# One-hot selection of the middle layers made by ScalarE in two steps, and the first block's factor held in PSUM, in a four-layer graph network

## The chip, the cores and the metric

The kernel runs on 1 core of one Trainium2 chip. The metric is the device time of one launch in microseconds (us). Engines are called by these names: PE (TensorE, matrix products), DVE (VectorE), ACT (ScalarE), POOL (GpSimd, which here issues the gathers of table rows) and SP (SyncE, plain DMAs).

## What is computed

A graph network of four layers over 3125 nodes (160 values each: 64 scalars and 32 vectors of 3) and 100000 edges, sorted by destination. Each layer normalises the nodes, looks up for each edge the row of a node, multiplies it by weights that a small network makes of the edge's attributes, and sums the messages over the edges that end at one node. The two middle layers are of one form; this is layer 2 (layer 1 has 8 attributes and no mean):

```
h = silu(edge_scalars @ (Wfc1 / sqrt(16)))
w = h @ (Wfc2 / sqrt(64));  w0, w1, w2, w3 = w[:, :64], w[:, 64:128], w[:, 128:160], w[:, 160:192]
e0, e1 = f0[edge_src], f1[edge_src]
sh0, sh1 = edge_attr_sh[:, :1], edge_attr_sh[:, 1:4]
mid0 = w0 * e0 * sh0
mid1 = w3 * einsum('eum,em->eu', e1, sh1) / sqrt(3)
mid2 = w1[:, :, None] * e0[:, :, None] * sh1[:, None, :]
mid3 = w2[:, :, None] * e1 * sh0[:, :, None]
n_k  = segment_sum(mid_k, edge_dst) / count
out  = sc + alpha * linear(n0..n3)
```

## The kernel before

Edges lie in tiles of 128 (one per partition); 4 tiles are a group, 2 tiles (half a group) are a unit whose destinations lie in one window of 128 nodes. Layer 0 runs 196 groups, then layers 1 and 2 run 208 groups each in a loop of their own (12 groups more than 196, for units that reach into a second window), then layer 3 has two passes. Between layers stand barriers of all engines. Everything is float32.

In the middle layers, for a group g:
- SP loads the edge attributes; POOL gathers 4 tiles of node rows from memory (`gathers_by_src`, line 567), up to 4 groups ahead (it waits until the messages of group g-4 are done).
- PE makes the hidden layer (`hidden_by_scalars`, line 1078, one product of 64x512) into bank 0; ACT takes it out with Silu (`hidden_out`, line 813); PE makes the weights w (`weights_by_hidden`, line 1092, four products of 192 columns) into PSUM, where each tile has 256 columns of which 192 are written.
- ACT multiplies the gathered rows by y0 (`rows_by_y0`, line 829, four instructions).
- DVE makes the one-hot selection (`select`: is the edge's place in its window equal to the column number, 128x512), the messages (`edges_by_window`, all recorded at line 1303), among them `t0` = w1 * e0 and the first block, `t0` times the three components of y (128x768), and adds the sums to the accumulator in SBUF (`add`).
- PE sums the messages over the window (`sums_by_window`, line 1111: per unit two products of selection and messages, 384 or 385 columns).

Each float32 product stands in the trace as two records, so 4 products of a group are x8.

The order of the work is written out by hand. `unrolled(count, [(lag, stage), ...])` runs, for each i, every stage on group i - lag, in the order of the list, and each engine executes its own list in order. The two lists that matter:

```
PE:  unrolled(ALL_GROUPS, [(0, sums_by_window(l)), (-2, weights_by_hidden(l)), (-3, hidden_by_scalars(l))])
ACT: unrolled(ALL_GROUPS, [(-1, rows_by_y0(l)), (-3, hidden_out(l))])
```

So in its turn i PE does the sums of group i, the weights of i+2 and the hidden layer of i+3; ACT does the rows of i+1 and takes out the hidden layer of i+3. Semaphores that the steps touch: `hidden_mm` (PE has made the hidden layer), `hidden_out` (ACT has taken it out), `weights_mm`, `rows_out`, `messages_done` (DVE), `sums_mm` (PE), `sums_added` (DVE), `got` (the gather has landed).

Of the kernel before, what the change touches and what calls it, by code (L numbers as in the profile page):

```python
# [87 lines left out]
def unrolled(count, stages):  # L88
    ahead, behind = min(lag for lag, _ in stages), max(lag for lag, _ in stages)
    for i in range(ahead, count + behind):  # L90
        for lag, stage in stages:
            if 0 <= i - lag < count:
                stage(i - lag)
# [7 lines left out]
def build(nc, a, out, layers=(0, 1, 2, 3)):  # L101
    with ExitStack() as ctx:
        def sb(name, shape, dt=F32):
            return ctx.enter_context(nc.sbuf_tensor(name, shape, dt))
# [27 lines left out]
        window_i = sb("window_i", [P, UNITS], I32)  # L132
        unit_i = sb("unit_i", [P, MORE], I32)
        column = sb("column", [P, P])
        put_i = sb("put_i", [P, TILES], I32)
        ident = sb("ident", [P, P])
        lower = sb("lower", [P, P])
# [45 lines left out]
        for l in (1, 2):  # L183
# [37 lines left out]
            "hid_free", "w_ready", "w_free", "weights_scaled", "msg_ready", "msg_free", "run_mm", "run_free",  # L221
            "run_ready",

            "scalars_in0", "scalars_in1", "hidden_mm", "hidden_out", "weights_mm", "rows_out", "messages_done",
            "sums_mm", "sums_added", "acc_zeroed", "acc_whole", "acc_turned", "acc_in_sbuf", "acc_mm", "acc_out",
            "p2_in0", "p2_in1", "p2_messages", "p2_mm", "p2_added",

# [45 lines left out]
        def window_views():  # L273
            g = carve()
            v = type("Windows", (), {})
            v.attr = g(2, 512)
            v.hid = g(2, 512)
            v.by_y0 = g(2, GROUP, DIM)
            v.msg = g(2, GROUP * 385)
            v.sel = g(2, GROUP, P)  # L280
            v.t0, v.t1, v.t2 = g(GROUP, S), g(GROUP, 3, V), g(GROUP, V)
            v.got = fore[:, 0:DEPTH * GROUP * DIM].rearrange("p (b t c) -> p b t c", b=DEPTH, c=DIM)
            return v

# [383 lines left out]
        def _(act):  # L668
# [148 lines left out]
            def rows_by_y0(l):  # L817
# [12 lines left out]
                    last.then_inc(s.rows_out, 1)  # L830
                return stage

            def post():

                def turned(j, b, first, half):

                    act.wait_ge(s.node_turned, 1)
                    act.sem_inc(s.node_turned, -1)
                    act.activation(Nv.hT[0:96, b, 0, :], bank[0:96, b, 0:128], ACT.Copy).then_inc(act_own, own.step())
                    act.activation(Nv.hT[:, b, 1:4, :], bank[:, b, 128:512].rearrange("p (i n) -> p i n", i=3),  # L840
                                   ACT.Copy).then_inc(s.node_in_sbuf, 1)
                    act.wait_ge(act_own, own.n)
                    act.sem_inc(act_own, own.reset())
                pipelined(act, SLOTS, [(0, turned)])

                o = fore[:, 0:SLOTS * 192].rearrange("p (j c) -> p j c", c=192)

                act.wait_ge(s.function_asked, 1)
                act.sem_inc(s.function_asked, -1)
                act.activation(skip[:, :, 0:96], o[:, :, 0:96], ACT.Sigmoid).then_inc(act_own, own.step())  # L850
                act.wait_ge(act_own, own.n)
                act.sem_inc(act_own, own.reset())
                act.sem_inc(s.function_done, 1)
# [37 lines left out]
            for l in (1, 2):  # L891
                prep(l)
                barrier(act, "act")
                unrolled(ALL_GROUPS, [(-1, rows_by_y0(l)), (-3, hidden_out(l))])
                barrier(act, "act")
                post_windows(l)
                barrier(act, "act")
# [69 lines left out]
        def _(pe):  # L967
# [129 lines left out]
            def sums_by_window(l):  # L1097
                f, at = SPEC[l]["f"], (l - 1) * ALL_GROUPS

                def stage(g):  # L1100
                    b = g % 2

                    pe.wait_ge(s.messages_done, at + g + 1)
                    for i in range(2):
                        u = 2 * g + i
                        if u >= 3:

                            pe.wait_ge(s.sums_added, 2 * at + u - 2)
                        o = bank[:, 5 + u % 3, 0:f]
                        for t in (2 * i, 2 * i + 1):  # L1110
                            last = nc.tensor.matmul(o, W.sel[:, b, t, :], W.msg[:, b, t * f:(t + 1) * f],  # L1111
                                                    start=t == 2 * i, stop=t == 2 * i + 1)
                        last.then_inc(s.sums_mm, 1)
                return stage
# [183 lines left out]
        def _(dve):  # L1298
# [46 lines left out]
            V_.tensor_copy(column[:], U.columnI).then_inc(dve_own, c.step())  # L1345
            V_.tensor_copy(spare[:], U.trashI[:, 0:1]).then_inc(dve_own, c.step())
            V_.memset(U.one, 1.0).then_inc(dve_own, c.step())
            dve.wait_ge(dve_own, c.n)

            dve.wait_ge(loaded, LOADS)  # L1350
# [172 lines left out]
            def select(g, to):  # L1523

                return tt(to, bc(in_window[:, g * GROUP:(g + 1) * GROUP], 2, P), bc(column[:], 1, GROUP), ALU.is_equal)
# [81 lines left out]
            def edges_by_window(l):  # L1607
# [11 lines left out]
                def stage(g):  # L1619
                    b = g % 2  # L1620
                    if g >= 2:

                        dve.wait_ge(s.sums_mm, 2 * at + 2 * g - 2)
                    select(g, W.sel[:, b]).then_inc(dve_own, c.step())
                    w, scaled = wmm(b), W.by_y0[:, b]
                    rows = W.got[:, g % DEPTH]
                    xs, xv = rows[:, :, 0:S], rows[:, :, S:DIM].rearrange("p t (i c) -> p t i c", c=V)
# [1 line left out]
                        W.msg[:, b, 0:GROUP * 384].rearrange("p (t c) -> p t c", c=384)  # L1629
                    blocks = msg[:, :, 96:384].rearrange("p t (i c) -> p t i c", c=96)  # L1630
                    yy = y[:, g * GROUP:(g + 1) * GROUP, :]
                    t0, t1, t2 = W.t0, W.t1, W.t2

                    if g >= 2:
                        add(2 * g - 3)
# [514 lines left out]
```

## Time and profile before

| what | us |
|---|---|
| median of 3 runs (9000.79 to 9057.08) | 9042.92 |
| the profiled execution, its own time | 9064.85 |
| its span, first to last instruction | 9063.1 |
| layer 1, from the first to the last hidden layer taken out (207 periods) | 1180.5 |
| layer 2, the same | 1189.1 |

The profile is of one execution. Durations of single instructions overlap at their ends: an engine starts the next before the last one's end is recorded. So the distance from start to start is what an instruction holds its engine for. [...]

### The profile page before, as it was taken

How to read it: one execution, taken by the hardware profiler on the slowest of the kernel's cores; microseconds unless marked ns; L12 is line 12 of the kernel's file. 1: busy time of each engine (PE TensorE's matmuls, PEld its weight loads, DVE VectorE, ACT ScalarE, POOL GpSimd, SP SyncE). 2: the span in 40 equal slices, each digit the busy share in tenths (PEclk: the TensorE clock that was granted, in tenths of full speed). 3: DMA queues.
4: the chain of work that ended last, by engine and by line, in shares of the span. 5: the costliest groups of instructions: out<-in, count | busy, mean ns of one | idle time of the engine just before them, and what ended most of it. 6: DMA issues, size and time to landing. Idle time of an engine off the chain costs nothing. (4 is left out here: it accounts for less than half of the span.)

```text
span 9063.1 us, 110799 instructions
## 1 busy us (share of the span) xinstructions
PE 7003.5 (77%) x30346; PEld 4677.3 (52%) x30346; DVE 6579.6 (73%) x18757; ACT 3111.1 (34%) x7975; POOL 6045.2 (67%) x4814
## 2 busy tenths in 40 slices
PE   3666666666664699999799999598989998986467
PEld 1222222222223455555455555388888888876455
DVE  4555555555554688877688887588999999987885
ACT  1222222222221333333333333265666666664000
POOL 0888888888883377776477776288888888885000
PEclk9777777777775699999799999598999999998787
DMA  5888888888886122222122222133332332222342
GB/s 171 130 130 128 128 127 128 128 129 129 129 129 153 46 64 60 59 60 50 41 65 63 63 63 51 38 79 79 82 82 82 83 84 82 82 80 61 96 131 85
DMA packets 486585, 826.92 MB, mean 91 GB/s; under 512 B 106849, under 2 KB 337846, under 8 KB 485718
## 3 DMA queue, kind: packets, MB, share of 16 engines
q0 software_dynamic: 305664, 547.66, 34.0%
q1 hardware_dynamic: 174406, 271.38, 9.5%
q8 instruction: 254, 4.16, 0.2%
q14 instruction: 357, 2.92, 0.1%
q10 hardware_dynamic: 5904, 0.79, 0.1%
HBM read 523.71 MB, written 295.72 MB: 90 GB/s over the span
## 5 line engine op out<-in xcount | busy, mean ns | idle before, releaser
L567 POOL DMA_INDIRECT fore<-node_table,src_i x1664 | 1884.4, 1132 | 666.7 <-issue 503.7
L1037 PE MATMUL bank<-work 128*128 128x480 f32 x1568 | 1124.3, 880 | 942.9 <-PEq L1036 935.9
L1303 DVE TENSOR_TENSOR work<-work 128x128 f32<-128x128 f32 (+4 forms) x4274 | 1599.8, 408 | 52.3 <-DVEq L1686 35.0
L616 POOL DMA_INDIRECT src_sum<-work,put_i x784 | 1309.9, 1671 | 245.0 <-issue 226.4
L1303 DVE TENSOR_TENSOR work<-work,y 128x384 f32<-128x384 f32 (+3 forms) x2964 | 1371.4, 506 | 59.0 <-ACT work L926 40.4
L567 POOL DMA_INDIRECT fore<-src_table,src_i x784 | 1076.6, 1373 | 431.5 <-issue 238.6
L1111 PE MATMUL bank<-work 128*128 128x384 f32 (+1 forms) x3328 | 1288.0, 533 | 82.1 <-DVE work L1303 80.9
L1037 PEld LDWEIGHTS bank<-work 128*128 128x128 f32 x1568 | 427.5, 292 | 1647.4 <-issue 1642.7
L1303 DVE TENSOR_TENSOR work<-bank,fore 128x256 f32<-128x256 f32 (+1 forms) x1004 | 447.4, 446 | 950.0 <-DMA fore<-node_table,dst_i 948.0
L567 POOL DMA_INDIRECT fore<-node_table,dst_i x784 | 821.5, 1048 | 433.9 <-issue 235.8
L567 POOL DMA_INDIRECT fore<-dst_table,dst_i x784 | 931.2, 1188 | 238.9 <-issue 238.9
L1111 PEld LDWEIGHTS bank<-work 128*128 128x128 f32 x3328 | 643.0, 203 | 807.9 <-issue 259.1
L1190 PE MATMUL bank<-ident,work 128*128 128x128 f32 x4704 | 704.0, 289 | 264.8 <-DVE work L1303 264.8
L1303 DVE TENSOR_TENSOR work<-work,bank 128x384 f32 (+6 forms) x2056 | 852.8, 423 | 68.3 <-issue 58.2
L1190 PEld LDWEIGHTS bank<-ident,work 128*128 128x128 f32 x4704 | 549.6, 147 | 384.2 <-DVE work L1303 313.4
L797 ACT ACTIVATE work<-bank 128x480 f32<-128x480 f32 x784 | 447.0, 570 | 694.6 <-ACTq L794 694.1
L829 ACT ACTIVATE work<-fore,y 128x160 f32<-128x160 f32 x1664 | 573.8, 416 | 317.3 <-DMA fore<-node_table,src_i 316.6
L813 ACT ACTIVATE work<-bank 64x512 f32<-64x512 f32 x416 | 245.7, 591 | 1268.4 <-PE bank L1078 1268.3
L1092 PE MATMUL bank<-w_fc,work 64*128 64x192 f32 x3328 | 657.6, 338 | 5.4 <-ACT work L813 5.4
L1092 PEld LDWEIGHTS bank<-w_fc,work 64*128 64x128 f32 x3328 | 534.3, 188 | 246.1 <-issue 234.0
L784 ACT ACTIVATE work<-bank 64x512 f32<-64x512 f32 x196 | 115.7, 590 | 1365.7 <-ACTq L783 1345.6
L1289 PE MATMUL bank<-work 128*128 128x164 f32 x1664 | 338.4, 358 | 188.5 <-DVE work L1303 187.7
(229 smaller groups left out, 12223.8 us busy)
## 6 DMA issues: line engine op xcount, KB each, us to landing
edge_h<-work SPq DMA_DIRECT2D x196, 320.0 KB
work<-edge_h SPq DMA_DIRECT2D x196, 320.0 KB, 2.9
fore<-node_table,src_i POOLq DMA_INDIRECT x1664, 2.7
work<-in_edge_attr SPq DMA_DIRECT2D x196, 128.0 KB
work<-src_keys SPq DMA_DIRECT2D x196, 128.0 KB
src_sum<-work SPq DMA_DIRECT2D x4, 6240.0 KB, 40.8
work<-src_sum SPq DMA_DIRECT2D x100, 240.0 KB, 3.3
fore<-node_table,dst_i POOLq DMA_INDIRECT x784
```

Of the source, the lines that this page charges most:

```text
L567: return pool.indirect_dma_start(dst, None, table, bass.IndirectOffsetOnAxis(ap=idx, axis=0), bounds_check=bound, oob_is_err=True)
L616: pool.indirect_dma_start(src_sum[t], bass.IndirectOffsetOnAxis(ap=put_i[:, e:e + 1], axis=0), E.run[:, g % 2, t * 480:(t + 1) * 480], Non ...
L784: act.activation(E.hid[0:64, b, :], bank[0:64, 7 * b, :], ACT.Relu).then_inc(s.hid_ready, 1)
L797: act.activation(E.run[:, b, t * f:(t + 1) * f], bank[:, 5 + (part * GROUP + t) % RUN_BANKS[0], 0:f], ACT.Copy).then_inc(act_own, own.step())
L813: act.activation(W.hid[0:64, b, :], bank[0:64, 0, :], ACT.Silu, scale=(8 ** -0.5, 0.25)[l - 1]).then_inc(s.hidden_out, 1)
L829: last = act.activation(W.by_y0[:, b, t, :], W.got[:, g % DEPTH, t, :], ACT.Copy, scale=y[:, e:e + 1, 0])
L1037: nc.tensor.matmul(bank[:, 5 + (part * GROUP + t) % RUN_BANKS[0], 0:f], E.sel[:, b, t, :], E.msg[:, b, t * f:(t + 1) * f], start=True, sto ...
L1092: last = nc.tensor.matmul(wmm(b)[:, t, 0:192], W.hid[0:64, b, t * P:(t + 1) * P], wt[f"fc2_{l}"][:], start=True, stop=True)
L1111: last = nc.tensor.matmul(o, W.sel[:, b, t, :], W.msg[:, b, t * f:(t + 1) * f], start=t == 2 * i, stop=t == 2 * i + 1)
L1190: last = nc.tensor.transpose(bank[:, to + t, i * P:(i + 1) * P], f[:, b, at + t, c0:c0 + P], ident[:])
L1289: last = nc.tensor.matmul(o, P2.sel[:, b, t, :], P2.msg[:, b, t, :], start=t == 2 * i, stop=t == 2 * i + 1)
L1303: return V_.tensor_tensor(o, p, q, op)
```

## The change

In the loops of layers 1 and 2 the DVE instruction `select` is taken out. ACT gets a stage `places` in its place, at lag 0 and first in its list: four Abs instructions make |place - column| for each of the 4 tiles into a new tile `away` (in spare room of the tile `fore`), ACT waits for its own four, and one Relu makes 1 - away of it, which is 1 where the two are equal and 0 elsewhere, into the selection `W.sel`. A new semaphore `places_out` says that it is made; PE waits for it before the sums of a group, and ACT before it writes `away` again. ACT waits on `sums_mm` before it overwrites a selection. `t0` no longer has a tile in SBUF: it is written into columns 192 to 255 of each tile's weights in PSUM and read from there by the first block's product. Layer 0 and layer 3 are as they were.

```diff
--- before.py
+++ after.py
@@ -132,6 +132,7 @@
         window_i = sb("window_i", [P, UNITS], I32)
         unit_i = sb("unit_i", [P, MORE], I32)
         column = sb("column", [P, P])
+        unity = sb("unity", [P, 1])
         put_i = sb("put_i", [P, TILES], I32)
         ident = sb("ident", [P, P])
         lower = sb("lower", [P, P])
@@ -221,7 +222,7 @@
             "hid_free", "w_ready", "w_free", "weights_scaled", "msg_ready", "msg_free", "run_mm", "run_free",
             "run_ready",
 
-            "scalars_in0", "scalars_in1", "hidden_mm", "hidden_out", "weights_mm", "rows_out", "messages_done",
+            "scalars_in0", "scalars_in1", "hidden_mm", "hidden_out", "weights_mm", "rows_out", "places_out", "messages_done",
             "sums_mm", "sums_added", "acc_zeroed", "acc_whole", "acc_turned", "acc_in_sbuf", "acc_mm", "acc_out",
             "p2_in0", "p2_in1", "p2_messages", "p2_mm", "p2_added",
 
@@ -278,7 +279,8 @@
             v.by_y0 = g(2, GROUP, DIM)
             v.msg = g(2, GROUP * 385)
             v.sel = g(2, GROUP, P)
-            v.t0, v.t1, v.t2 = g(GROUP, S), g(GROUP, 3, V), g(GROUP, V)
+            v.t1, v.t2 = g(GROUP, 3, V), g(GROUP, V)
+            v.away = fore[:, DEPTH * GROUP * DIM:DEPTH * GROUP * DIM + GROUP * P].rearrange("p (t n) -> p t n", t=GROUP)
             v.got = fore[:, 0:DEPTH * GROUP * DIM].rearrange("p (b t c) -> p b t c", b=DEPTH, c=DIM)
             return v
 
@@ -830,6 +832,24 @@
                     last.then_inc(s.rows_out, 1)
                 return stage
 
+            def places(l):
+                at = (l - 1) * ALL_GROUPS
+
+                def stage(g):
+                    b = g % 2
+                    if g >= 2:
+
+                        act.wait_ge(s.sums_mm, 2 * (at + g - 1))
+                    if g:
+
+                        act.wait_ge(s.places_out, at + g)
+                    for t in range(GROUP):
+                        e = g * GROUP + t
+                        act.activation(W.away[:, t, :], column[:], ACT.Abs, bias=in_window[:, e:e + 1], scale=-1.0).then_inc(act_own, own.step())
+                    act.wait_ge(act_own, own.n)
+                    act.activation(W.sel[:, b], W.away, ACT.Relu, bias=unity[:], scale=-1.0).then_inc(s.places_out, 1)
+                return stage
+
             def post():
 
                 def turned(j, b, first, half):
@@ -891,7 +911,9 @@
             for l in (1, 2):
                 prep(l)
                 barrier(act, "act")
-                unrolled(ALL_GROUPS, [(-1, rows_by_y0(l)), (-3, hidden_out(l))])
+                unrolled(ALL_GROUPS, [(0, places(l)), (-1, rows_by_y0(l)), (-3, hidden_out(l))])
+                act.wait_ge(act_own, own.n)
+                act.sem_inc(act_own, own.reset())
                 barrier(act, "act")
                 post_windows(l)
                 barrier(act, "act")
@@ -1099,6 +1121,8 @@
 
                 def stage(g):
                     b = g % 2
+
+                    pe.wait_ge(s.places_out, at + g + 1)
 
                     pe.wait_ge(s.messages_done, at + g + 1)
                     for i in range(2):
@@ -1345,6 +1369,7 @@
             V_.tensor_copy(column[:], U.columnI).then_inc(dve_own, c.step())
             V_.tensor_copy(spare[:], U.trashI[:, 0:1]).then_inc(dve_own, c.step())
             V_.memset(U.one, 1.0).then_inc(dve_own, c.step())
+            V_.memset(unity[:], 1.0).then_inc(dve_own, c.step())
             dve.wait_ge(dve_own, c.n)
 
             dve.wait_ge(loaded, LOADS)
@@ -1621,7 +1646,6 @@
                     if g >= 2:
 
                         dve.wait_ge(s.sums_mm, 2 * at + 2 * g - 2)
-                    select(g, W.sel[:, b]).then_inc(dve_own, c.step())
                     w, scaled = wmm(b), W.by_y0[:, b]
                     rows = W.got[:, g % DEPTH]
                     xs, xv = rows[:, :, 0:S], rows[:, :, S:DIM].rearrange("p t (i c) -> p t i c", c=V)
@@ -1629,7 +1653,7 @@
                         W.msg[:, b, 0:GROUP * 384].rearrange("p (t c) -> p t c", c=384)
                     blocks = msg[:, :, 96:384].rearrange("p t (i c) -> p t i c", c=96)
                     yy = y[:, g * GROUP:(g + 1) * GROUP, :]
-                    t0, t1, t2 = W.t0, W.t1, W.t2
+                    t0, t1, t2 = w[:, :, 192:256], W.t1, W.t2
 
                     if g >= 2:
                         add(2 * g - 3)
```

ACT, in the loop of layer 1, before (the names behind "waits" are semaphores; x3 is three more of the same):

```order
L813 ACTIVATE work<-bank 64x512 [waits weights_mm,hidden_mm]
L829 ACTIVATE work<-fore,y 128x160 [waits messages_done,got1_3]
L829 ACTIVATE work<-fore,y 128x160 x3
L813 ACTIVATE work<-bank 64x512 [waits weights_mm,hidden_mm]
L829 ACTIVATE work<-fore,y 128x160 [waits messages_done,got1_0]
L829 ACTIVATE work<-fore,y 128x160 x3
```

ACT at the same place in the changed kernel (L815 is the old L813, L831 the old L829, L848 and L850 are the new stage):

```order
L815 ACTIVATE work<-bank 64x512 [waits weights_mm,hidden_mm]
L848 ACTIVATE fore<-column,in_window 128x128 [waits places_out,sums_mm]
L848 ACTIVATE fore<-column,in_window 128x128 x3
L850 ACTIVATE work<-fore,unity 128x512 [waits act_own]
L831 ACTIVATE work<-fore,y 128x160 [waits messages_done,got1_3]
L831 ACTIVATE work<-fore,y 128x160 x3
L815 ACTIVATE work<-bank 64x512 [waits weights_mm,hidden_mm]
```

The new stage of group i+1 stands between the taking out of the hidden layer of group i+3 and the rows of group i+2.

PE in the changed kernel, one turn and the start of the next (before, the same rows without `places_out`, at lines 1111, 1092 and 1078):

```order
L1135 MATMUL bank<-work 128x384 [waits sums_added,messages_done,places_out]
L1135 MATMUL bank<-work 128x384
L1135 MATMUL bank<-work 128x384 [waits sums_added]
L1135 MATMUL bank<-work 128x384
L1114 MATMUL bank<-w_fc_1,work 128x192 [waits messages_done,hidden_out]
L1114 MATMUL bank<-w_fc_1,work 128x192 x3
L1100 MATMUL bank<-work,w_fc_1 64x512 [waits hidden_out,scalars_in1]
L1135 MATMUL bank<-work 128x384 [waits sums_added,messages_done,places_out]
```

Nothing moved on PE; the first product of the sums has one wait more, and it stands right behind the hidden layer's product (L1100).

## Rows read from the trace of the kernel before

**Rows 1.** The page: busy time of the engines, and POOL and clock in 40 slices.
```profile
PE 7003.5 (77%) x30346; PEld 4677.3 (52%) x30346; DVE 6579.6 (73%) x18757; ACT 3111.1 (34%) x7975; POOL 6045.2 (67%) x4814
...
POOL 0888888888883377776477776288888888885000
PEclk9777777777775699999799999598999999998787
```
**Rows 2.** Windows: length, busy PE, PEld, DVE, ACT, POOL; clock, DMA share, GB/s.
```profile
500.00:2500.00 2000.00, 1267.56 (x2700) 568.31 (x2699) 1111.68 (x4050) 430.33 (x751) 1634.12 (x1201) 0.76 0.81 128
3078.60:4259.10 1180.50, 1140.69 (x3710) 619.38 (x3710) 966.18 (x2261) 396.68 (x1032) 929.41 (x825) 0.95 0.25 61
4428.60:5617.70 1189.10, 1150.56 (x3711) 623.51 (x3712) 968.76 (x2264) 398.22 (x1032) 937.67 (x826) 0.95 0.26 63
```
**Rows 3.** Timeline of one undisturbed turn of layer 1: start, us, engine, instruction.
```profile
3240.42 2.85 PE L1111 MATMUL bank<-work 128*128 128x384 f32 x8
...
3243.20 1.56 PE L1092 MATMUL bank<-w_fc,work 64*128 64x192 f32 x8
...
3244.69 1.07 PE L1078 MATMUL bank<-work,w_fc 8*64 8x512 f32 x2
...
3245.69 2.85 PE L1111 MATMUL bank<-work 128*128 128x384 f32 x8
...
3245.79 0.59 ACT L813 ACTIVATE work<-bank 64x512 f32<-64x512 f32 x1 [3.41 <-PE bank L1078]
...
3246.29 1.37 ACT L829 ACTIVATE work<-fore,y 128x160 f32<-128x160 f32 x4
```
**Rows 4.** Groups by line and shape, layer 1's loop, 3078.6 to 4259.1 us.
```profile
L567 POOL DMA_INDIRECT fore<-node_table,src_i x825 | 930.8, 1128 | 251.4 <-issue 250.2 <-DVE work L1303 1.2
...
L829 ACT ACTIVATE work<-fore,y 128x160 f32<-128x160 f32 x824 | 284.1, 416 | 148.3 <-DMA fore<-node_table,src_i 148.0
...
L1303 DVE TENSOR_TENSOR work<-work,y 128x768 f32<-128x768 f32 x206 | 196.3, 953 | 0.0
L1303 DVE TENSOR_TENSOR work<-in_window,column 128x512 f32<-128x512 f32 x205 | 140.9, 687 | 4.2 <-PE bank L1111 3.9
L813 ACT ACTIVATE work<-bank 64x512 f32<-64x512 f32 x207 | 122.3, 591 | 633.7 <-PE bank L1078 633.7
```
**Rows 5.** Timeline of DVE and POOL: a long gather and the next.
```profile
3390.11 0.95 DVE L1303 TENSOR_TENSOR work<-work,y 128x768 f32<-128x768 f32 x1
3390.38 1.56 POOL L567 DMA_INDIRECT fore<-node_table,src_i  x1 [0.30 <-issue]
...
3392.24 1.01 POOL L567 DMA_INDIRECT fore<-node_table,src_i  x1 [0.30 <-issue]
```
**Rows 6.** Groups over the whole span: ACT with short and with wide operands.
```profile
L926 ACT ACTIVATE work<-work,y 128x64 f32<-128x64 f32 x784 | 228.9, 347 | 0.0
...
L764 ACT ACTIVATE work<-bank 64x128 f32<-64x128 f32 x75 | 20.3, 271 | 53.5 <-ACTq L761 53.1
```
**Rows 7.** PE's sums behind a wait, in layers 1 and 2, and the clock at the first.
```profile
3806.55 1.07 PE L1078 MATMUL bank<-work,w_fc 8*64 8x512 f32 x2
3809.26 4.35 PE L1111 MATMUL bank<-work 128*128 128x384 f32 x8 [1.64 <-DVE work L1303]
...
4801.79 4.54 PE L1111 MATMUL bank<-work 128*128 128x385 f32 x8 [2.62 <-DVE work L1303]
...
3808.90:3812.30 3.40, 3.04 (x5) 1.83 (x6) 3.40 (x10) 1.39 (x4) 2.79 (x3) 0.50 0.29 72
```
**Rows 8.** PE in layer 0: one turn of the timeline, and groups from 500 to 2500 us.
```profile
1522.27 5.39 PE L1037 MATMUL bank<-work 128*128 128x480 f32 x8 [5.50 <-PEq L1036]
1527.59 1.78 PE L1022 MATMUL bank<-w_fc,work 64*128 64x224 f32 x8
1529.29 1.07 PE L1010 MATMUL bank<-work,w_fc 64*64 64x512 f32 x2
...
L1010 PE MATMUL bank<-work,w_fc 64*64 64x512 f32 x300 | 160.3, 614 | 0.0
```

## The prediction

> **What bounds the kernel now.** I read the page first, then the windows of the three loops, then one turn of the timeline with the groups by line beside it, and last the order of the instructions. The page shows PE and DVE busy over the whole run and POOL near the top in the middle of it [rows 1]; such shares are averages over loops with different limits, so they decide nothing. The windows do: in the loops of layers 1 and 2 PE is busy 1140.7 of 1180.5 us and 1150.6 of 1189.1 us, at a granted clock of 0.95 [rows 2]. There are 207 periods in each, so one turn takes 1180.5 / 207 = 5.70 us and 1189.1 / 207 = 5.74 us.
>
> The timeline of an undisturbed turn says what a turn is made of [rows 3]. PE starts the sums at 3240.42, the weights at 3243.20 (2.78 us later), the hidden layer at 3244.69 (1.49) and the next sums at 3245.69 (1.00): 5.27 us, with no gap. PE is the bound of such a turn. POOL is as near: four gathers of 1.01 us with 0.30 us between them are 5.25 us, and over the loop a gather takes 1.128 us on average [rows 4], 4 x (1.128 + 0.304) = 5.73 us, which is the measured turn. So the floor is PE's 5.27, and the 0.45 us above it come from gathers that last longer than 1.01. DVE is not the bound: it waits for gathers and for ACT, and PE has its input in time in most turns.
>
> What matters most for the change is where ACT stands. It takes out the hidden layer (L813) 0.03 us after PE's product for it ends (3244.69 + 1.07 = 3245.76, then 3245.79), and PE has then already begun the next sums [rows 3]. Today nobody waits for what ACT does there: its output is needed a turn later.
>
> **The change part by part.**
>
> *DVE loses the selection*, 0.687 us per group [rows 4], 208 groups in each of two layers, 286 us of DVE's time. DVE is off the path, so by itself this is worth 0.
>
> *The first block's factor in PSUM.* The 128x768 product takes 0.953 us [rows 4] and reads one operand from PSUM afterwards. Its price stays between 0 and +0.1 us, on an engine with slack: I take 0.
>
> *POOL's long gathers.* A gather that starts 0.27 us after the 128x768 product lasts 1.56 us where the next one lasts 1.01 [rows 5]. That product has both inputs in SBUF, and so has the selection; the change takes one input out of SBUF and the other instruction off DVE. If all long gathers go, a turn falls from 5.70 to PE's 5.27. That is a gain only where POOL still sets the turn, and after the next paragraph it does not.
>
> *ACT gets five instructions, and PE a wait.* This is the part that decides. In its turn PE does sums(i), weights(i+2), hidden(i+3). ACT takes out hidden(i+3), and only then comes places(i+1), because the new stage stands first in the next turn of its list. The next thing on PE is sums(i+1), and it now waits for places(i+1). So the ring is closed: PE's hidden(i+3), ACT's Silu on it, four Abs, Relu, then PE's sums(i+1), weights, hidden(i+4). What used to lie beside PE's 2.78 us of sums now lies ahead of them, in each turn, and behind the waiting product on PE stand the weights and the hidden layer, which ACT's next turn waits for. No look-ahead of the loop helps, since it is the order on the two engines that makes the ring.
>
> The length of ACT's part: 0.03 us to start; 0.50 us until the next instruction can start behind the Silu (3245.79 to 3246.29 [rows 3]). Four Abs of 128 columns with an operand per partition: the nearest row is L829, four in 1.37 us at 160 columns [rows 3]; from 64 columns (347 ns [rows 6]) to 160 (416 ns [rows 4]) a column costs 0.72 ns, so 32 columns fewer save 0.023 us each, 1.28 us for four. The cheap end is L764, 0.271 us for 128 columns without such an operand [rows 6]: with overlap about 0.8 us for four; the dear end is no overlap, 4 x 0.416 = 1.66 us. Relu over 512 columns: at least L813's 0.591 us [rows 4], at most about 0.8; from 416 ns with 352 columns more at 0.72 ns comes 0.67, and I take 0.70. Two steps between semaphores (ACT's wait on its own Abs, PE's start) at about 0.06 us each, a little above the 0.03 that ACT needs behind PE. Sum: 0.03 + 0.50 + 1.28 + 0.06 + 0.70 + 0.06 = 2.63 us. Ends: 2.05 and 3.2 us.
>
> *PE's own work gets slower as well.* It now idles 2.63 us in each turn. [...] A loop that has a wait in every turn is layer 0's: clock 0.76 over 2000 us [rows 2]. There the hidden product has 300 records, 2 a group, so 150 groups, 13.33 us and 1267.56 / 150 = 8.45 us of PE busy per group [rows 2, 8]. At full clock its work would be 2.85 x 480/384 = 3.56 us for the sums, 1.70 for the weights (start to start) and 1.07, together 6.3 [rows 3, 8]. So a wait per turn costs it 2.15 us of slower products. Layer 0 is the nearest case of a repeated wait, and I take its 2.15 us per turn for the new loop. Ends: 0 (the clock stays at the upper level) and 5.27 (all work at the lower level takes twice as long).
>
> **Sum.** A turn is 2.63 + 5.27 + 2.15 = 10.05 us. Two loops of 207 periods: 414 x 10.05 = 4161 us in place of 1180.5 + 1189.1 = 2369.6 us, which is +1791 us. The profiled execution took 9064.85 us, so it would take 10,856 us; the median of the runs shown is 22 us below that execution, which gives 10,834. All other stages keep their time. I forecast 10,840 us, 20% slower.
>
> **Rivals.**
>
> *Faster: the wait is covered and only the relief of POOL is left.* The mechanism: places(i+1) is made before PE ends hidden(i+3), and gathers fall to 1.01 us. Then the turn is PE's 5.27 to 5.28 us: 414 x 5.28 = 2186, 184 us less, 8,860 us. For it: the long gathers in rows 5, and that ACT is busy only 397 of 1180 us [rows 2]. It would decide if the selection were made a turn ahead of its use. Against it: in the order ACT's new stage stands directly behind the wait for hidden(i+3), and PE's next product waits for it. Chance 0.02. [...]
>
> *Nothing measurable*, the relief and a shorter wait cancelling: this needs a turn of 5.6 to 5.9 us, so a wait under 0.6 us, while the Silu alone holds ACT for 0.50 and the Relu 0.59. Chance 0.02.
>
> *Slower, but PE keeps its full clock.* The turn is 2.63 + 5.27 = 7.90 us: 414 x 7.90 = 3271, +901, 9,944 us. For it: PE's busy share would be two thirds, and some waits in layer 1 are shorter than here. Against it: rows 7, where idle times of 1.64 and 2.62 us were enough. Chance 0.12. [...]
>
> *Slower, and PE stays at the lower level.* Its work is at most 10.54 us, the turn 13.17: +3083, 12,126 us. For it: the ring leaves PE idle in every turn. Against it: in layer 0, with a wait of 5.50 us, the weights and the hidden layer behind the sums are back at full speed (1.78 and 1.07 us [rows 8], as 1.07 in rows 3). Chance 0.08.
>
> **How the numbers follow.** The forecast has 0.76, the full clock 0.12, the low clock 0.08, faster 0.02, nothing 0.02. About 1% is what a measurement of this kernel can tell from no change. Faster by over 1%: 0.02; within 1%: 0.02; slower: 0.96. The range: at the low end ACT's part is 2.05 us and the slower products cost the 1.5 us of rows 7, 8.82 us a turn, +1282, 10,325 us; at the high end ACT's part is 3.2 us and half of PE's work is at the lower level, 2.63 us more, 11.10 us a turn, +2226, 11,270 us. I take 10,310 to 11,280.
>
> **What would show it.** In the profile after: PE idle once per turn, ahead of L1135, for about 2.6 us, released by ACT's L850; the distance from one L815 to the next near 10 us; a clock of about 0.7 in both loops; four Abs in about 1.3 us; gathers of 1.01 us throughout, with POOL waiting for DVE's messages instead of issuing steadily. The forecast is wrong if PE's wait is not there or ends with another engine (then the ring was misread), if L1135 stays near 2.85 us (clock) or if DVE or a gather ends the waits of PE.

## The result and the profile after

The changed kernel took 10,918.83 us (median of 4 runs, 10,914.12 to 10,924.01), against 9,046.54 us for the kernel before (median of 4 on the same chip). The ratio is 1.2085, with a 95% interval of 1.2048 to 1.2122: 21% slower. Forecast were 10,840 us in a range of 10,310 to 11,280.

The page of the changed kernel, engines and slices, to be read beside [rows 1]:

```profile
PE 7853.0 (72%) x30346; PEld 5063.3 (46%) x30346; DVE 6451.3 (59%) x18342; ACT 3875.1 (35%) x10055; POOL 5854.7 (54%) x4814
...
POOL 2888888888233333333233433431788888888100
PEclk9777777777566666666666666666889999999787
```

PE has the same 30346 records and is busy 850 us longer: the same work, done more slowly. POOL fell from 7 tenths to 3 in the middle; it now waits. The windows of the two loops (length; busy PE, PEld, DVE, ACT, POOL; clock, DMA share, GB/s), beside [rows 2]. The clock is the share that the profile shows as granted to TensorE, averaged over the window. The traces have two levels of it: the turn of [rows 3], 3240.42 to 3245.69 us, stands at the upper one (1.00), the sums of [rows 7] at the lower (0.50).

```profile
500.00:2500.00 2000.00, 1264.10 (x2697) 567.52 (x2697) 1111.97 (x4050) 430.23 (x748) 1634.69 (x1198) 0.76 0.81 128
3083.10:5191.50 2108.40, 1573.77 (x3710) 819.69 (x3710) 906.69 (x2062) 771.90 (x2056) 842.28 (x829) 0.67 0.14 34
5361.50:7471.60 2110.10, 1575.65 (x3710) 819.23 (x3710) 909.06 (x2062) 771.81 (x2057) 842.31 (x829) 0.67 0.15 36
```

The loops took 2108.4 and 2110.1 us in place of 1180.5 and 1189.1, together +1848.9 us. The spans differ by 10916.3 - 9063.1 = 1853.2 us, so all but 4 us of the loss is in these loops. Layer 0's stretch reads as before.

One turn of the timeline, beside [rows 3] (start, us, engine, instruction; in brackets the idle time ahead and who ended it):

```profile
3500.80 1.07 PE L1100 MATMUL bank<-work,w_fc 8*64 8x512 f32 x2
...
3501.91 0.59 ACT L815 ACTIVATE work<-bank 64x512 f32<-64x512 f32 x1 [6.46 <-PE bank L1100]
...
3502.40 1.26 ACT L848 ACTIVATE fore<-column,in_window 128x128 f32<-128x128 f32 x4
...
3503.70 0.72 ACT L850 ACTIVATE work<-fore,unity 128x512 f32<-128x512 f32 x1
3504.32 1.37 ACT L831 ACTIVATE work<-fore,y 128x160 f32<-128x160 f32 x4
3504.47 5.15 PE L1135 MATMUL bank<-work 128*128 128x384 f32 x8 [2.60 <-ACT work L850]
...
3509.55 1.56 PE L1114 MATMUL bank<-w_fc,work 64*128 64x192 f32 x8
```

This is the ring, link by link: PE's hidden product ends at 3501.87, ACT starts at 3501.91, Abs at 3502.40, Relu at 3503.70 until 3504.42, PE at 3504.47 after 2.60 us idle, released by L850. The recorded end of an instruction can lie behind the start of the next: L815 is recorded until 3502.50 and the Abs start at 3502.40, L850 until 3504.42 and L831 starts at 3504.32; in [rows 3] the sums run until 3243.27 and the weights start at 3243.20. So the parts of a turn are counted from start to start. The sums then take 5.15 us where [rows 3] have 2.85. The weights and the hidden layer behind them take 1.56 and 1.07 us, as in [rows 3]. The next L815 starts at 3512.14: the turn is 10.24 us. In both loops the turns from the 5th to the 95th percentile are all 10.24 us (start of L815 to the next, 414 distances); the few short ones, 5.49 us the shortest, bring the mean to 10.19. The windows show the clock inside such a turn, 0.50 from 3502.30 us to the end of the sums and 0.99 behind them:

```profile
3502.30:3509.10 6.80, 4.63 (x7) 2.52 (x8) 1.93 (x6) 3.36 (x10) 1.22 (x3) 0.50 0.12 27
3509.10:3512.50 3.40, 3.01 (x12) 1.46 (x10) 2.44 (x5) 0.35 (x1) 2.79 (x3) 0.99 0.24 52
```

The groups by line of layer 1's loop, beside [rows 4], and two lines of the view of waits (who waited for whom: us in total, times, longest):

```profile
L1135 PE MATMUL bank<-work 128*128 128x384 f32 x1640 | 1053.5, 821 | 533.3 <-ACT work L850 533.3
L569 POOL DMA_INDIRECT fore<-node_table,src_i x829 | 843.2, 1017 | 1248.1 <-DVE work L1327 1055.6 <-issue 192.4
...
L848 ACT ACTIVATE fore<-column,in_window 128x128 f32<-128x128 f32 x820 | 259.0, 388 | 0.0
...
L1327 DVE TENSOR_TENSOR work<-bank,y 128x768 f32<-128x768 f32 x207 | 196.8, 951 | 0.0
L850 ACT ACTIVATE work<-fore,unity 128x512 f32<-128x512 f32 x205 | 147.9, 722 | 6.7
```
```profile
PE bank L1135 <- ACT work L850: 533.3, 205, 2.6
DVE work L1327 <- PE bank L1135: 495.7, 409, 2.0
```

533.3 us over 205 turns are 2.60 each, always for L850. Gathers are at 1.017 us on average in place of 1.128, and POOL idles 1056 us until DVE is done with a group: the relief of POOL has come, on an engine that no longer sets the turn. DVE also waits for PE's sums now, which come late; with the ring open, in the run at 0.9814 below, that wait is not among its larger ones.

### The profile page after: what moved, and what is told of

It reads as the page before. It is cut to its first block and busy times, and to the rows that moved or that the text cites. A ratio compares the mean times of both kernels' runs of the same rounds, so it can differ in the third digit from the quotient of the medians.

```text
span 10916.3 us, 112903 instructions
## 1 busy us (share of the span) xinstructions
PE 7853.0 (72%) x30346; PEld 5063.3 (46%) x30346; DVE 6451.3 (59%) x18342; ACT 3875.1 (35%) x10055; POOL 5854.7 (54%) x4814
## 5 line engine op out<-in xcount | busy, mean ns | idle before, releaser
L569 POOL DMA_INDIRECT fore<-node_table,src_i x1664 | 1692.6, 1017 | 2659.5 <-DVE work L1327 2113.0
L1135 PE MATMUL bank<-work 128*128 128x384 f32 (+1 forms) x3328 | 2130.2, 817 | 1072.6 <-ACT work L850 1071.6
L1135 PEld LDWEIGHTS bank<-work 128*128 128x128 f32 x3328 | 1042.2, 328 | 2194.8 <-ACT work L850 1436.4
L1059 PEld LDWEIGHTS bank<-work 128*128 128x128 f32 x1568 | 426.6, 292 | 1652.7 <-issue 1648.7
L815 ACT ACTIVATE work<-bank 64x512 f32<-64x512 f32 x416 | 246.2, 592 | 2661.4 <-PE bank L1100 2661.4
L1327 DVE TENSOR_TENSOR work<-bank,work 128x256 f32<-128x256 f32 x832 | 405.1, 487 | 1323.1 <-ACT work L831 1323.1
L1327 DVE TENSOR_TENSOR work<-work,y 128x384 f32<-128x384 f32 (+2 forms) x2548 | 972.7, 432 | 54.8 <-ACT work L948 36.2
L1327 DVE TENSOR_TENSOR work<-bank,fore 128x256 f32<-128x256 f32 (+1 forms) x588 | 271.0, 461 | 951.3 <-DMA fore<-node_table,dst_i 951.3
L831 ACT ACTIVATE work<-fore,y 128x160 f32<-128x160 f32 x1664 | 569.1, 412 | 0.0
```

The costliest lines, as they stand in the source:

```text
L569: return pool.indirect_dma_start(dst, None, table, bass.IndirectOffsetOnAxis(ap=idx, axis=0), bounds_check=bound, oob_is_err=True)
L815: act.activation(W.hid[0:64, b, :], bank[0:64, 0, :], ACT.Silu, scale=(8 ** -0.5, 0.25)[l - 1]).then_inc(s.hidden_out, 1)
L831: last = act.activation(W.by_y0[:, b, t, :], W.got[:, g % DEPTH, t, :], ACT.Copy, scale=y[:, e:e + 1, 0])
L1059: nc.tensor.matmul(bank[:, 5 + (part * GROUP + t) % RUN_BANKS[0], 0:f], E.sel[:, b, t, :], E.msg[:, b, t * f:(t + 1) * f], start=True, sto ...
L1327: return V_.tensor_tensor(o, p, q, op)
```

## The experiments

Theory: the loss is the ring of PE's hidden product, ACT's Silu, four Abs and Relu, and PE's sums, plus what PE's lower clock costs because of the wait. Rivals: ACT's added load itself, the writing into PSUM, or slow sums for another reason than the clock. The runs fell on five chips, here A to E in order of time; where an expectation speaks of the first, second or third call, it means chips A, B and C. On A and C the kernel before was itself slower, 9,411 and 9,585 us; this is told at the runs that it touches. The runs on chip B, and the one with PE kept busy on C, are single runs, so their times are read for large effects only and their turns from the trace.

### Where the selection stands

One line, the place of the stage on ACT:

```diff
-unrolled(ALL_GROUPS, [(0, places(l)), (-1, rows_by_y0(l)), (-3, hidden_out(l))])
+unrolled(ALL_GROUPS, [(-1, rows_by_y0(l)), (-1, places(l)), (-3, hidden_out(l))])
```

> The changed kernel with ACT's new stage moved: it makes the selection of group i+1 in turn i, behind the rows of group i+1 and ahead of taking out the hidden layer of i+3. The same instructions, another place. Theory (the loss is the ring PE hidden product, ACT Silu, Abs and Relu, PE sums): the ring is open, PE waits for ACT no longer, its clock comes back to 0.95 or more, and with the relief of POOL the turn is 5.28 us: 414 x 5.28 = 2186 us for the two loops in place of 2370 before, 8,860 to 8,900 us, 2% faster than before. Rival (the load on ACT itself, five more instructions, is the cost): ACT has 4 us of work per turn in a turn of 5.3 either way, so the time stays well above before, over 9,300 us.

It took 9,528 us, beside 9,411 for the kernel before on that chip (A): ratio 1.013 (1.010 to 1.017). The 21% were gone, but so was the gain. By its number the rival was met (over 9,300 us), but the kernel before is over 9,300 us there too, so the number doesn't tell theory from rival. The profile has gathers of 1.02 us and turns with a mean of 6.31 us, in which three engines start late at the same moment behind PE (SP's transfer, not shown, starts at 3502.50 as well; "remote" stands where the profile finds no releaser):

```profile
3497.67 1.07 PE L1100 MATMUL bank<-work,w_fc 8*64 8x512 f32 x2
3498.66 2.85 PE L1135 MATMUL bank<-work 128*128 128x384 f32 x8
...
3502.46 0.43 DVE L1327 TENSOR_TENSOR bank<-bank,fore 128x256 f32<-128x256 f32 x1 [4.47 <-remote]
3502.50 0.59 ACT L815 ACTIVATE work<-bank 64x512 f32<-64x512 f32 x1 [5.21 <-remote]
```

DVE waits for weights and ACT for the hidden layer, which PE's records show as made by 3498.74. The ends of PE's records are modelled, so that the signal and not the product was late is a reading of them. I counted the turns in which L815 starts over 1 us after both PE's record and ACT's own last instruction ended: 107 of 416 here, and 2 of 416 (the table load at each loop's start) in the kernel before and in the changed kernel. All counts of late turns below hold these two.

> The selection one turn ahead, once more: in the first call both this kernel and the one before lost some 350 us to stalls of 3 to 12 us in which ACT, DVE and SP got PE's signals late together, so the chip and not the kernel was measured; the run of the kernel before in the second call had none. Theory (ring open, gathers relieved): turn 5.28 us in most turns, mean gather 1.02 us, 8,860 to 8,920 us, ratio 0.98 to 0.99. Rival (the relief of POOL is worth nothing, since the long turns have another cause): gathers at 1.02 us and still a mean turn of 5.6 us, ratio 0.995 to 1.005.

It met such a chip again (C): 9,603 against 9,585 us, ratio 1.0032 (1.0013 to 1.0051), 118 late turns. By its number the rival was met again, but its turn of 5.6 us was not (6.32). By what was laid down ahead of the third run, such a ratio says nothing between theory and rival. The third time, on chip D, there were none beyond the two table loads:

> The selection one turn ahead, a third time, to meet a chip without the late signals. On the two chips of the calls before, the kernel before took 9411 and 9585 us and not 9047; layer 0's loop kept its 2559 us, the loops with a busy PE got longer. Theory (ring open, gathers relieved): where the kernel before takes 9,000 to 9,150 us, this one has a turn of 5.28 us in most turns, a mean gather of 1.02 us, and a ratio of 0.98 to 0.99. Rival (the relief of POOL is worth nothing): mean turn 5.6 us, ratio 0.995 to 1.005. If the signals come late again (the kernel before over 9,300 us), the ratio says nothing between the two.

8,878.88 us against 9,048.53, ratio 0.9814 (0.9787 to 0.9841). The same instructions as in the changed kernel, in another order, are 1.9% faster than before instead of 21% slower, on this chip; on A and C they were 1.3 and 0.3% slower than the kernel before. Windows of its two loops and its timeline:

```profile
3078.90:4183.20 1104.30, 1098.33 (x3711) 602.48 (x3712) 842.12 (x2062) 774.24 (x2062) 840.91 (x829) 0.99 0.27 65
4348.30:5453.50 1105.20, 1099.37 (x3711) 601.63 (x3711) 841.89 (x2062) 774.17 (x2061) 842.75 (x829) 0.99 0.28 68
```
```profile
3502.07 0.59 ACT L815 ACTIVATE work<-bank 64x512 f32<-64x512 f32 x1 [1.48 <-PE bank L1100]
3502.57 1.37 ACT L831 ACTIVATE work<-fore,y 128x160 f32<-128x160 f32 x4
...
3503.84 1.26 ACT L848 ACTIVATE fore<-column,in_window 128x128 f32<-128x128 f32 x4
...
3505.14 0.72 ACT L850 ACTIVATE work<-fore,unity 128x512 f32<-128x512 f32 x1
...
3507.23 2.23 PEld L1135 LDWEIGHTS bank<-work 128*128 128x128 f32 x8 [0.81 <-issue]
```

The Relu ends at 3505.86, 1.4 us before PE's next sums, and ACT then still waits 1.48 us for PE. PE is busy 1098 of 1104 us, at a clock of 0.99, 5.33 us a turn. ACT's load is the same as in the changed kernel (774 against 772 us per loop), so the load is not the cost: that rival falls. The place is.

### The two parts apart

The factor in PSUM alone, in the kernel before:

```diff
-t0, t1, t2 = W.t0, W.t1, W.t2
+t0, t1, t2 = w[:, :, 192:256], W.t1, W.t2
```

> The kernel before with one part of the change alone: the factor t0 stands in PSUM columns 192 to 255; DVE still makes the selection. Theory (POOL's gathers are held up by DVE instructions with two SBUF inputs, and set what a turn takes above PE's 5.27 us): the 128x768 product stops holding gathers up, the selection still does, so the mean gather falls from 1.128 us to between 1.02 and 1.10, the turn from 5.72 to 5.30 to 5.60 us, the time by 50 to 170 us, to 8,870 to 9,000 us. Rival (access to PSUM costs DVE or PE time): the 128x768 product gets longer than 0.953 us by 0.1 or more and the time stays within 30 us of before or grows.

> The factor t0 in PSUM alone, again, with the kernel that makes the selection one turn ahead on the same chip. Theory (gathers held up by DVE instructions with two SBUF inputs set the turn above 5.27 us): mean gather 1.06 us, half of the gain of the other kernel, ratio 0.985 to 0.997. Rival: ratio 0.997 to 1.003 with the same gathers.

The first run was on the slow chip A (9,437 against 9,411 us, ratio 1.002, 0.9995 to 1.0044, 91 late turns): by its number the rival's time (within 30 us of before), though the product stayed at 0.95 us and the mean gather fell to 1.057 us, as forecast. The second, on chip D beside the run at 0.9814, took 8,898.59 us: ratio 0.9823 (0.9797 to 0.985). One line brings the whole gain. I had expected half of it. That long gathers held up the kernel before is in its waits for a gather to land, and in those of this run (us in total, times, longest):

```profile
DVE work L1303 <- DMA fore<-node_table,src_i: 153.7, 117, 6.6
```
```profile
DVE work L1303 <- DMA fore<-node_table,src_i: 6.6, 1, 6.6
```

The gain has two parts. From the kernel before to the run at 0.9814, PE's idle time in layer 1 falls from 39.8 to 6.0 us and its busy time from 1140.7 to 1098.3, with the clock going from 0.95 to 0.99: products behind a wait had run at the lower clock. [rows 7] show two such waits, and 0.50 at the first; over both loops of the kernel before, all 18 waits of 1.5 to 3 us ahead of the sums were followed by sums of over 3.2 us.

ACT's selection one turn ahead with `t0` in SBUF (the same one line undone, its tile put back):

> As the run with the selection one turn ahead, but with t0 in SBUF as before: ACT's selection alone, without the PSUM columns. Theory: the selection no longer holds gathers up, the 128x768 product still does; since long gathers were seen behind that product, the gain is the smaller part: mean gather 1.05 to 1.12 us, turn 5.35 to 5.65 us, 8,900 to 9,010 us. Rival (the selection's place on DVE did all the harm): as fast as with both parts, 8,860 to 8,900 us.

> ACT's selection alone, one turn ahead, with t0 in SBUF, again: the fourth corner beside the kernel before, t0 in PSUM alone (ratio 0.982) and both (0.981). In the first call its gathers took 1.076 us on average against 1.055 with t0 in PSUM alone and 1.023 with both. Theory (gathers matter only until POOL is as fast as PE): POOL needs 4 x (1.076 + 0.304) = 5.52 us a turn, so about 5.5 us a turn and 9,047 - 414 x 0.18 = 8,970 us, ratio 0.988 to 0.996. Rival (either relief is enough by itself): ratio 0.979 to 0.985. If the kernel before takes over 9,300 us, the ratio says nothing between the two.

On the slow chip A 9,478 us, ratio 1.0063 (1.0039 to 1.0088), 79 late turns, and neither theory nor rival by its number. On chip E 8,863.65 us against 9,019.74, ratio 0.9833 (0.9787 to 0.988): again the whole gain, and the rival of that run holds. The gathers of layer 1's loop in the three kernels, in the order both, `t0` alone, selection alone, one line each:

```profile
L569 POOL DMA_INDIRECT fore<-node_table,src_i x829 | 841.6, 1015 | 258.4 <-issue 241.8 <-DVE work L1327 16.6
```
```profile
L567 POOL DMA_INDIRECT fore<-node_table,src_i x828 | 851.9, 1029 | 252.5 <-issue 251.0 <-DVE work L1303 1.5
```
```profile
L569 POOL DMA_INDIRECT fore<-node_table,src_i x827 | 845.1, 1022 | 252.1 <-issue 239.2 <-DVE work L1327 12.9
```

All three are close to 1.01 us, against 1.128 in [rows 4], and the mean turns are 5.33, 5.33 and 5.33 us (layer 1). So with either part POOL keeps up with PE, and a second relief adds nothing. In the third kernel the 128x768 product still has both inputs in SBUF, and gathers are hardly lengthened. My estimate for it had come from gathers of 1.076 us on the slow chip, where the engines fell out of step; the undisturbed loop does better. The traces show why. In both kernels a gather that started while the 128x768 product with both inputs in SBUF ran ended, in most cases, about 0.89 us after the product did, so it was longer by nearly all that was left of the product. In layer 1 of the kernel before 160 gathers started inside it, with 0.65 us left on average, and took 1.55 us; in the third kernel 77 did, with 0.22 us left, and took 1.10, since in its undisturbed turns a gather starts just ahead of the product:

```profile
3503.39 1.01 POOL L569 DMA_INDIRECT fore<-node_table,src_i  x1 [0.30 <-issue]
3503.43 0.95 DVE L1327 TENSOR_TENSOR work<-work,y 128x768 f32<-128x768 f32 x1
```

With `t0` in PSUM (the kernel with both) 175 started inside the product and none took over 1.02 us. So the gain of the selection alone came from where gathers start, and of the two parts only the PSUM operand took the conflict inside this product away.

The changed kernel with `t0` back in SBUF:

> The changed kernel with t0 back in SBUF: ACT's selection at its place, without the PSUM columns. Theory (the ring sets the turn, DVE and POOL have slack in it): PE waits 2.6 us per turn for the Relu, the turn stays 10.24 us, the time is that of the change within 0.5%. Rival (writing t0 into PSUM is part of the loss): the time falls by 1% or more.

10,889.76 us, one run on chip B, 0.3% under the changed kernel's median on another chip, gathers of 1.029 us, and a turn of 10.24 us. The records of L1135 are the same within 1 us (1054.1 us in 1640, 821 ns each), with the same 533.3 us of waiting for L850. The PSUM columns have no part in the loss. On chip B the kernel before was also run for its own profile:

> The kernel before, unchanged, for a profile on the chip of the experiments, where it was 4% slower than in the runs shown (9411 against 9047 us). If the extra time lies in stages that the change doesn't touch, the turns of layers 1 and 2 stay at 5.7 us and the rest grows by 365 us; if it lies in long turns, their median stays at 5.27 us and their mean goes to 6.1 or more.

It took 9,012.83 us, with turns of 5.65 us in layer 1 (median 5.27) and no late turn beyond the two table loads; a second run there took 9,140.55 us. So it met a chip that isn't slow, and its question, where the kernel before loses time on chip A, was not answered: no profile of it on a slow chip is kept.

### The length of the ring

A shorter one, without the four Abs (this kernel leaves out the distance |place - column|, so its selections are not the reference's):

```diff
-for t in range(GROUP):
-    e = g * GROUP + t
-    act.activation(W.away[:, t, :], column[:], ACT.Abs, bias=in_window[:, e:e + 1], scale=-1.0)...
-act.wait_ge(act_own, own.n)
```

The wait and the reset of ACT's own count behind the loop, which the Abs needed, went with them (not shown).

> The changed kernel without the four Abs instructions (the selection is then 1 minus whatever stands in the tile, so the messages are summed wrongly; all products keep their size). ACT's part of the ring is 0.03 + 0.50 + 0.72 + 0.06 = 1.3 us in place of 2.60. Theory: PE's wait falls to 1.3 us; if the clock stayed up the turn would be 6.6 us, with waits of this length as costly as before (1.5 us) 8.1: I expect 6.6 to 8.6 us, 9,400 to 10,250 us. Rival (the turn is fixed by something else than the ring's length, such as DVE waiting for the rows): the turn stays within 3% of 10.24 us.

9,801.05 us, one run. The timeline:

```profile
3507.17 0.59 ACT L815 ACTIVATE work<-bank 64x512 f32<-64x512 f32 x1 [4.15 <-PE bank L1094]
3507.66 0.71 ACT L846 ACTIVATE work<-fore,unity 128x512 f32<-128x512 f32 x1
...
3508.42 2.85 PE L1129 MATMUL bank<-work 128*128 128x384 f32 x8 [1.29 <-ACT work L846]
...
3515.05 5.49 PE L1129 MATMUL bank<-work 128*128 128x384 f32 x8 [1.29 <-ACT work L846]
```

PE's wait is 1.29 us as worked out. The median turn of layer 1 is 6.63 us, which is 1.29 + 5.27 and a remainder of 0.07; from 3508.42 to 3513.70 us, the rest of the turn shown, the clock is 1.00. The mean is 7.49 us: after a wait of the same length the sums take 2.85 us in 256 of 414 turns and 4.3 to 5.5 us in nearly all others, so behind a wait of 1.3 us the clock fell some of the time (0.86 over the loop, 0.50 from 3515.05 to 3520.50 us, the sums of 5.49 us).

A longer one, the Relu made twice:

```diff
+act.activation(W.sel[:, b], W.away, ACT.Relu, bias=unity[:], scale=-1.0).then_inc(act_own, own.step())
+act.wait_ge(act_own, own.n)
 act.activation(W.sel[:, b], W.away, ACT.Relu, bias=unity[:], scale=-1.0).then_inc(s.places_out, 1)
```

> The changed kernel with the Relu made twice (the same result), the second behind a wait for the first: ACT's part of the ring is 2.60 + 0.72 + 0.06 = 3.4 us. Theory in its simple form (turn = ACT's part + PE's work + 2.3 us of slower products): the turn is 11.0 us and the time 320 us over that of the change. Its other form, since the turn was 10.24 us in nearly all turns with the clock alternating in step: a longer wait takes up time that the lower clock would have cost, the turn stays at 10.24 us while PE's wait grows to 3.4, and the mean clock rises above 0.67.

10,969.56 us, one run, 0.5% over the changed kernel; 47 of these 51 us lie outside the two loops. The window of layer 1's loop, and the sums of one turn:

```profile
3082.90:5195.50 2112.60, 1423.59 (x3710) 761.32 (x3710) 895.45 (x2062) 919.71 (x2262) 840.76 (x829) 0.83 0.14 34
```
```profile
3509.20 4.39 PE L1137 MATMUL bank<-work 128*128 128x384 f32 x8 [3.35 <-ACT work L852]
```

PE waits 3.35 us, 0.75 more than in the changed kernel, and the sums take 4.39 us, 0.76 less. The turn stays 10.24 us, and the loop is 4 us longer (2112.6 against 2108.4). The simple form of the theory (11.0 us a turn) is refuted, its other form holds: the added wait took up time that the lower clock had cost, and the mean clock went from 0.67 to 0.83.

### The clock

Three products that nobody reads, put into PE's wait:

```diff
+if g >= 2:
+    pe.wait_ge(s.sums_added, 2 * at + 2 * g - 2)
+    for _ in range(3):
+        nc.tensor.matmul(bank[:, 5 + 2 * g % 3, 0:384], ident[:], x[:]...[:, 0:384], start=True, stop=True)
 pe.wait_ge(s.places_out, at + g + 1)
```

> The changed kernel with three more products on PE in each turn from the third on, 128x384 columns each, of the identity and the node features into the bank that the next sums overwrite, ahead of the wait for the selection: 2.1 us of work that nobody reads, in a wait of 2.6. Theory (of the 10.24 us 2.3 are the lower clock's): PE is idle 0.5 us per turn, the granted clock goes to 0.95 or more, the turn falls to 2.6 + 5.3 = 7.9 us, the time to about 9,950 us although PE does more. Rival (the sums are slow for another reason than the clock, or the clock doesn't come back): the turn stays at 10.24 us or gets longer.

The windows and a turn:

```profile
3083.30:4729.30 1646.00, 1541.55 (x4929) 815.23 (x4929) 888.42 (x2062) 771.84 (x2056) 857.41 (x829) 0.99 0.18 44
```
```profile
4006.63 2.20 PE L1128 MATMUL bank<-x,ident 128*128 128x384 f32 x6
4006.74 0.59 ACT L815 ACTIVATE work<-bank 64x512 f32<-64x512 f32 x1 [4.15 <-PE bank L1100]
...
4009.30 2.85 PE L1141 MATMUL bank<-work 128*128 128x384 f32 x8 [0.47 <-ACT work L850]
```

The idle time is 0.47 us, the clock 0.99, the sums are back at 2.85 us, and the turn is 7.94 to 7.96 us (5th to 95th percentile). PE does 2.1 us more per turn, and the turn is 2.30 us shorter: the difference between 5.15 and 2.85. So of the 4.5 us that the change added to a turn, 2.3 are the lower clock's. The whole run took 10,315 us, more than the 9,950 expected, because this was the slow chip C: its two loops took 1646.0 and 1651.7 us, close to the 207 x 7.95 of the theory, and the excess lies elsewhere. Layer 3's first pass took 2799 us there, 2753 in the other kernel on that chip, and 2451 in the kernel before on chip B, while layer 0's loop took 2559 to 2560 us in all three. What picks the loops that get longer is not shown: PE is busy 63% of layer 0's stretch, which kept its time, and 86% of layer 3's first pass here, but 94% of the two loops here, which came out as forecast, while with the selection one turn ahead the same loops took 1306 to 1327 us each on the slow chips and 1104 to 1105 on D.

## Why the prediction was right

- **The ring.** Forecast: PE waits once per turn, ahead of L1135, for L850. Measured: 205 waits in layer 1, all for L850. Shown by moving that one stage (0.9814 against 1.2085).
- **ACT's part**, 2.63 us forecast, 2.60 measured: Silu 0.49 start to start (0.50), four Abs 1.26 (1.28), Relu 0.72 (0.70), two signals 0.04 and 0.05 (0.06 each). The rows of other ACT instructions, scaled by columns, were enough.
- **PE's slower products**, 2.15 us forecast from layer 0, 2.30 measured, and shown to be the clock's by keeping PE busy. That the sizes agree is in part luck. Layer 0's 2.15 stands behind a wait of 5.50 us and larger sums, and the term changes with the wait: 4.39 - 2.85 = 1.54 us behind 3.35 us, 7.49 - 6.63 = 0.86 on average behind 1.29. It was the largest of the small misses. The 1.5 us at the low end of the range stand in [rows 7] against [rows 3]: 4.35 - 2.85 behind a wait of 1.64 us, and 4.54 - 2.85 = 1.69 behind 2.62. The high end lets work at the lower clock take twice as long, and the products of the sums do: most start 0.32 us apart in the turn of [rows 3] (clock 1.00), and 0.64 in the changed kernel from 3505.27 us on (0.50).
- **The turn**, 10.05 us forecast, 10.19 measured on average (2108.4 / 207 and 2110.1 / 207). The two loops took 4218.5 us where 4161 were forecast; these 57 us are most of the 79 by which the time was missed. The high end of ACT's part, 3.2 us, is 3.11 by its own terms, which would put the upper bound some 40 us lower and changes nothing.
- **DVE's lost selection and the factor in PSUM**, 0 forecast. Holds: with `t0` back in SBUF the turn is the same. The 128x768 product takes 951 ns with an operand in PSUM, 953 before; the 0 to 0.1 us set aside for it were an estimate with no row behind it, and this is its measure.
- **POOL's relief.** Forecast to be real and worth nothing here. The gathers fell to 1.017 us, POOL waits. With the ring open the relief is worth what that rival was priced at: 8,860 us forecast, 8,879 measured. The traces show gather by gather where the long ones stood: in layer 1 of the kernel before, those that started inside the 128x768 product with both inputs in SBUF took 1.55 us on average (160 of them), those inside the selection 1.18 (27); with one input of the product in PSUM, in the same layer of the run at 0.9814, none inside it took over 1.02. With the selection alone gone the mean was 1.022 us: the 77 inside the product that remained still took 1.10 on average, but most gathers now start outside it.
- **The floor of the kernel before.** The 0.45 us above 5.27 were put down to long gathers alone. In layer 1 some 0.2 us of each turn, (1140.7 - 1098.3) / 207, were the slower products behind the waits that the gathers caused.
- **The two clock rivals.** The clock neither stayed up nor stayed down: behind the idle time of 2.60 us it was 0.50 at the sums and 0.99 at the weights and the hidden layer, 0.67 over each loop.
- **What the working did not see.** It added the wait and the slower products as if they were independent. The run with two Relus shows that they are not: from a wait of 2.60 to one of 3.35 us their sum stayed, and each changed. At 1.29 us the sum was smaller, so this holds between these two runs and no further.

## What to carry to other kernels

Work taken from a full engine and given to one that is a third busy still lands on the path if it is put behind a wait for the engine that needs it next: read from both engines' lists what stands between "released by" and "waited for", before counting load. Make such work one turn ahead, behind what that engine has to deliver and ahead of its next wait; here this one line turned 21% slower into 2% faster on a chip without the late starts. And a wait on PE can be paid twice, when the products behind it run at the lower clock (0.50 here): a wait of 2.60 us in each turn cost 2.30 us more, one of 1.29 us 0.86, one of 0.47 us nothing.

## What was not expected of the hardware

- The turn kept 10.24 us while ACT's part grew from 2.60 to 3.35 us, and with 1.29 us it fell to 6.63 in most turns. Shortening the wait from 3.35 to 2.60 us brought the two loops nothing (4223 against 4219 us), and the next 1.3 us brought the kernel 10%.
- Three useless products of 0.7 us each made the turn 2.3 us shorter, by keeping the clock at 0.99.
- A gather that started inside a 128x768 DVE product with both inputs in SBUF took up to 1.87 us, and 1.01 when it started 0.04 us ahead of it. The same conflict was there in both kernels; where in the turn gathers start decided what it cost.
- On two of the chips ACT, DVE and SP started 1 to 12 us after PE's records had ended (the median of each run is 2.2 to 3.6 us), 77 to 116 times in the two loops beside the two table loads, in kernels whose PE was busy 90 to 94% of these loops there, at a clock of 0.90 to 0.92; in the kernel with the three useless products, on one of the same chips, it was twice. The kernel before was 4 and 6% slower there. It has no profile on those chips; the kernels that have one lost part of their time outside these two loops. On such a chip a gain of 2% read as a loss of 1.3%. What delays the starts stays open.
